# A decoder layer with eight experts: the gate threshold search with one clamping instruction a round, twenty held results, and the second half of the experts written out

## What is computed

```python
probs = jax.nn.softmax(xf @ Wr, axis=-1)              # 1792 tokens, 8 experts
topk_probs, topk_experts = jax.lax.top_k(probs, 2)
cap = 560                                             # max(ceil(1792*2*1.25/8), 1)
for e in range(8):
    mask = topk_experts == e
    gate = jnp.sum(jnp.where(mask, topk_probs, 0.0), axis=-1)
    g_masked = jnp.where(jnp.any(mask, axis=-1), gate, -jnp.inf)
    vals, idx = jax.lax.top_k(g_masked, cap)          # only the 560 largest gates stay
    g = jnp.where(jnp.isfinite(vals), vals, 0.0)
    h = jax.nn.relu(xf[idx] @ W1[e]) @ W2[e]          # 128 -> 512 -> 128
    y = y.at[idx].add(g[:, None] * h)
```

## Time and profile before

| | us |
|---|---|
| three runs | 1064.82, 1067.64, 1068.8 |
| median | 1067.64 |
| the profiled execution, its own time | 1067.1 |
| its span in the trace | 1065.4 |
| attention stages, up to the first product of part 0 | 865.6 |
| parts 0 to 63 | 101.2 |
| parts 64 to 127 | 77.7 |
| from the end of part 127 to the end of the span | 21.0 |

### The profile page before, as it was taken

How to read it: one execution, slowest core, us unless ns; L and a number is a source line. 1 busy time by engine, 2 the same in 40 slices (tenths; PEclk the granted TensorE clock), 3 DMA queues, 4 the chain that set the end, 5 groups by cost and what they waited for, 6 DMA issues and landing times.

```text
span 1065.4 us, 29427 instructions
## 1 busy us (share of the span) xinstructions
PE 991.5 (93%) x10672; PEld 801.4 (75%) x10672; DVE 726.2 (68%) x1428; ACT 633.0 (59%) x1026; POOL 354.7 (33%) x325
## 2 busy tenths in 40 slices
PE   6579999999999999999999999999977978999993
PEld 5345788877888778887788877888756767888993
DVE  3776777776777767777677777777721357767896
ACT  3214777777777777777777777777750033444551
POOL 7315333233332333323333233332200151117742
PEclk9757999999999999999999999999995568999997
DMA  4068556665566655666556665566401010004301
GB/s 95 0 129 176 126 111 139 150 142 111 108 143 145 142 112 108 143 145 143 111 108 144 144 143 109 108 148 143 103 2 42 1 40 20 21 1 158 126 34 35
DMA packets 41431, 109.57 MB, mean 103 GB/s; under 512 B 15075, under 2 KB 23590, under 8 KB 41382
## 3 DMA queue, kind: packets, MB, share of 16 engines
q1 hardware_dynamic: 41382, 108.93, 45.8%
HBM read 31.32 MB, written 0.97 MB: 30 GB/s over the span
## 4 chain that ended last, share of the span: by engine, by line
PE 79%; DVE 6%; POOL 5%; issue 5%; DMA 2%; SPq 1%; ACT 1%; POOLq 0%; DVEq 0%; ACTq 0%
PE psum L1050 16%; PE psum L1036 16%; PE psum L1100 12%; PE psum L1075 8%; PE psum L1084 8%; PE psum L1104 4%; PE psum L1167 3%; POOL OS_all L517 3%; PE psum L1195 2%; PE psum L1196 1%; PE psum L1197 1%; DMA arena<-gate_rows 1%; PE psum L1063 1%; PE psum L1168 1%; PE psum L1206 1%
## 5 line engine op out<-in xcount | busy, mean ns | idle before, releaser
L739 DVE TENSOR_REDUCE arena<-psum 128x1 f32<-128x500 f32 x672 | 445.4, 672 | 196.8 <-PE psum L1036 196.7
L562 ACT ACTIVATE arena<-psum 125x896 f32<-125x896 f32 x384 | 347.6, 915 | 98.4 <-PE psum L1050 90.3
L1036 PE MATMUL psum<-K_hi,Q_bd 128*128 128x500 f32 x672 | 321.9, 490 | 6.3 <-DVE arena L739 3.5
L461 POOL TENSOR_TENSOR arena<-arena,K_hi 128x500 fp32r<-128x500 f32 x96 | 123.9, 1292 | 395.8 <-ACT K_hi L577 394.8
L1050 PEld LDWEIGHTS psum<-Q_st,K_st 97*125 97x125 f32 x1536 | 220.7, 188 | 31.0 <-issue 11.2
L1050 PE MATMUL psum<-Q_st,K_st 97*125 97x224 f32 x1536 | 240.5, 279 | 3.1 <-issue 1.6
L1036 PEld LDWEIGHTS psum<-K_hi,Q_bd 128*128 128x128 f32 x672 | 130.4, 195 | 57.1 <-issue 28.3
L1100 PE MATMUL psum<-arena 125*25 125x168 f32 x3072 | 169.5, 310 | 0.2
L624 ACT ACTIVATE K_st<-psum 128x448 fp32r<-128x448 f32 x128 | 69.6, 544 | 89.8 <-PE psum L1197 89.4
L1104 PE MATMUL psum<-arena 125*9 125x56 f32 x3072 | 117.1, 213 | 0.0
L1104 PEld LDWEIGHTS psum<-arena 125*9 125x9 f32 x3072 | 94.4, 91 | 15.3
(11 more groups left out here) (245 smaller groups left out, 1104.1 us busy)
## 6 DMA issues: line engine op xcount, KB each, us to landing
K_st<-K_hi SPq DMA_DIRECT2D x256, 187.5 KB, 4.6
K_st<-arena SPq DMA_DIRECT2D x128, 187.5 KB, 3.4
arena<-in_ctx SPq DMA_DIRECT2D x32, 562.5 KB, 6.7
arena<-gate_rows SPq DMA_DIRECT2D x8, 896.0 KB, 4.5
arena<-in_L_ffn_W SPq DMA_DIRECT2D x16, 256.0 KB, 3.6
Q_st<-max_row SPq DMA_DIRECT2D x224, 0.5 KB, 1.7
arena<-K_st SPq DMA_DIRECT2D x12, 224.0 KB, 5.0
out<-x_all SPq DMA_DIRECT2D x4, 224.0 KB, 2.5
```

The costliest lines, as they stand in the source:

```text
L461: g.tensor_tensor(low.bitcast(F32R), low, K_hi[:, par, n * KB:n * KB + KB].bitcast(F32), ALU.subtract).then_inc(F["keys_low"], 1)
L562: a.activation(P2[c % NP].rearrange("p (n k) -> p n k", n=2), psum[0:CK, 2 + 2 * (c % 2):4 + 2 * (c % 2), 0:HQ // 2], ACT.Exp)\
L739: v.reduce_max(mx[:, n // NB, n % NB:n % NB + 1], bank_of(n)[:, 0:KB], AX.X).then_inc(F["piece_max_taken"], 1)
L1036: mm(bank_of(n)[:, 0:KB], Q_bd[:, p].rearrange("p h q -> p (h q)")[:, 128 * (n // NB):128 * (n // NB) + 128], K_hi[:, p, (n % NB) * KB:(n ...
```

## The change

**Constants.** `EARLY` is 13 and `BETWEEN` 49, so the gates are turned at part 13, and the rounds lie on parts 13 to 61: 17 rounds with two parts and 15 with one. There are `KEEP` = 20 places for results, four of them in a new array.

**Search.** `expert_rows` holds 4.0 instead of 1.0. A product of `ones` with the new array `level` fills 33 columns of bank 6 ahead of part 0 with minus four times 559.5; the product of round r is added to column r, so its sign says whether the count reaches the capacity. While the count is on its way, VectorE works out the two values that the candidate can take (`bounds`; two instructions in the first seven rounds, one in the next 23) into `low_high`, and when the sum is there, one instruction (max, then min with the two columns) gives the next candidate. The low parts of a round are moved one round later: behind the count of round r stand `low_parts(r - 1)`. The parts of the last round stand behind the count of equal gates, and the product for these (L1226, now L1273) stands behind part 63. Four small instructions that fill `signed` are new between the top two and the search.

**Experts.** All 32 units are written out on all engines. GpSimd splits the weights of experts 0 to 5 ahead of the first gating, those of expert 6 ahead of gating number 8 and of expert 7 ahead of number 18; SyncE loads the weights of experts 0 to 6 ahead of the gates. VectorE has no addition in units 16 to 18; the 30 additions of results 0 to 29 stand in units 19 to 31, two or three a unit, each behind one low part. The last two results are gated by VectorE itself, straight from PSUM, with no copy by ScalarE.

**End.** TensorE turns quad 0 ahead of the last `down` and quad 1 in the middle of it. VectorE's order is: statistics 0, gate and add result 30, scale 0, statistics 1, gate and add result 31, scale 1, statistics 2, scale 2, statistics 3, scale 3.

The core of the diff:

```diff
-EARLY, BETWEEN = 10, 46
+EARLY, BETWEEN = 13, 49
+KEEP = 20
+GATED = UNITS - 2
+WEIGHT = 4.0
+ADD_FROM = 19
...
+        more_results = at(128, KEEP - UNITS // 2, QC)
...
-            for e in range(NE - 2):
+            for e in range(NE - 1):
                 load_weights(e, e % 2)
...
-                if e in (1, 2):
-                    load_weights(NE - 3 + e, (NE - 3 + e) % 2)
+                if e == 1:
+                    load_weights(NE - 1, (NE - 1) % 2)
...
-            for e in range(NE // 2):
+            for e in range(NE - 2):
                 split_weights(e, e % 2, e // 2 + 1)
...
+            for n in range(GATED):
+                if n in (8, 18):
+                    e = NE - 2 if n == 8 else NE - 1
+                    split_weights(e, e % 2, e // 2 + 1)
+                e = n // NQ
+                pool.wait_ge(G_[e % 2], (e // 2 + 1) * 16)
+                pool.wait_ge(S4["result_copied"], n + 1 + PRIME)
+                g.tensor_tensor(held(n), held(n), gates[e % 2][:, n % NQ], ALU.mult).then_inc(S4["result_gated"], 1)
...
-                if not isinstance(u, int) or u >= UNITS // 2:
-                    act.wait_ge(S4["result_added"], u - (UNITS // 2 - 1) + PRIME)
-                a.activation(results[:, bass.ds(slot, 1)], bank[4 + p][:, 0:QC].unsqueeze(1), ACT.Copy).then_inc(S4["result_copied"], 1)
+                if u >= KEEP:
+                    act.wait_ge(S4["result_added"], u - KEEP + 1 + PRIME)
+                a.activation(held(u), bank[4 + u % 2][:, 0:QC], ACT.Copy).then_inc(S4["result_copied"], 1)
...
-            def count(op, where):
+            def count(op, where, bounds=None):
+                r = rounds[0]
                 v.tensor_scalar(gscr[:], G[:], where, 0.0, op, ALU.add, accum_out=cnt[:, 0:1]).then_inc(S4["counted"], 1)
-                for n in low_parts(rounds[0]):
+                if bounds:
+                    bounds()
+                for n in low_parts(r - 1) if r else ():
                     low_part(n // FC, n // FC, n % FC)
...
             for s in range(23):
-                bit, less = bits[:, s:s + 1], bits[:, min(s + 1, 22):min(s + 1, 22) + 1]
-                tot = count(ALU.is_ge, cand[:])
-                step(v.tensor_scalar(fac[:], tot, float(CAP), bit, ALU.is_ge, ALU.mult))
-                step(v.scalar_tensor_tensor((cand if s < 22 else thr)[:], fac[:], less, cand[:], ALU.subtract, ALU.add))
+                def bounds():
+                    last_of(v.tensor_scalar(low_high[:], offsets[:, s], cand[:], None, ALU.add))
+                tot = count(ALU.is_ge, cand[:], bounds)
+                step(v.tensor_scalar((cand if s < 22 else thr)[:], tot, low_high[:, 0:1], low_high[:, 1:2], ALU.max, ALU.min))
...
             v.tensor_copy(cnt[:, 1:2], pref[:, TT - 1:TT]).then_inc(S4["equal_counted"], 1)
+            for n in low_parts(ROUNDS - 1):
+                low_part(n // FC, n // FC, n % FC)
...
+            def gate(n):
+                dve.wait_ge(G_[1], 16 * (NE // 2))
+                dve.wait_ge(S4["result_made"], n + 1 + PRIME)
+                v.tensor_tensor(held(n), bank[4 + n % 2][:, 0:QC], gates[1][:, n % NQ], ALU.mult).then_inc(S4["result_gated"], 1)
+
+            def due(u):
+                return (u + 1 - ADD_FROM) * GATED // (UNITS - ADD_FROM) if u >= ADD_FROM - 1 else 0
+            for u in range(UNITS // 2, UNITS):
+                waiting = iter(range(due(u - 1), due(u)))
                 for f in range(FC):
-                    low_part(u, k, f)
...
+                    low_part(u, u, f)
+                    for n in islice(waiting, 1):
+                        add(n)
...
+            statistics(0)
+            gate(GATED)
+            add(GATED)
+            scale(0)
+            statistics(1)
+            gate(GATED + 1)
+            add(GATED + 1)
+            scale(1)
+            for n in range(2, NQ):
+                statistics(n)
+                scale(n)
...
-                        mm(bank[6][:, 0:1], expert_rows[:], cnt[:, 0:1], start=True, stop=True).then_inc(S4["total_made"], 1)
+                        mm(bank[6][:, rounds:rounds + 1], expert_rows[:], cnt[:, 0:1], start=False, stop=True, skip_group_check=True).then_inc(S4["total_made"], 1)
...
-                    if rounds == ROUNDS and u * FC + f == low_parts(ROUNDS - 1).stop + 3:
+                    if rounds == ROUNDS and u * FC + f == low_parts(ROUNDS - 1).stop + 1:
...
+            added(0)
             for f in range(FC):
                 down(UNITS - 1, UNITS - 1, f, 1)
...
+                if f == 1:
+                    added(1)
+            for n in range(2, NQ):
+                added(n)
```

More of the change, by code:

```diff
@@ L309, in bank_of @@
             return bank[0 if n == 0 else (n + 1) % 2]
-        def experts_after(eng, unit):
-            with eng.Fori(0, NE // 4) as i:
-                for k in range(2 * NQ):
-                    unit(i * (2 * NQ) + (UNITS // 2 + k), k)
         def has(b, ahead):
@@ L896, in count @@
                 rounds[0] += 1
[L897 to L906 removed]
+                dve.wait_ge(dve_step, done[0])
@@ L1210, in _, with added @@
             pe.wait_ge(S4["x_split"], NQ + PRIME)
+            mm(bank[6][:, 0:ROUNDS + 1], ones[:], level[:], start=True, stop=True).then_inc(S4["level_set"], 1)
             rounds = 0
-            for u in range(UNITS // 2):
+            def added(n):
+                pe.wait_ge(S4["result_added"], UNITS - NQ + n + 1 + PRIME)
+                for t in range(QT):
+                    last = t_.transpose(bank[(6, 7, 0, 1)[n]][0:TT, D * t:D * t + D], y_sum[:, n, TT * t:TT * t + TT], ident[:])
+                last.then_inc(S4["outputs_made"], 1)
+            for u in range(UNITS):
                 for f in range(FC):
```

109 lines of the change are left out of this document (50 added, 59 removed).

## The result

The changed kernel takes 1055.36 us (median of 4 runs, 1053.86 to 1056.22), against 1067.13 for the kernel before beside it: a ratio of 0.989, 95% interval 0.9867 to 0.9912. Timed once more with the last experiments it gave 1054.13 us and 0.990 (0.9868 to 0.9928). The forecast was 1056.5 in a range of 1053 to 1061.5.

What follows compares the result with a forecast made beforehand. TensorE alone was taken to bound parts 64 to 127, with the search costing it 26 us before; terms -1.0 -3.7 -3.6 +0.6 -3.5 +0 +0.5 +0.15 = -10.6 from 1067.1 gave 1056.5 us, range 1053 to 1061.5.

Steps and rivals of the forecast that it cites:

- stall ahead of turning: TensorE's wait before the gates are turned: three fewer steps behind the last low part, 2.49 to about 1.5 us, -1.0.
- clock behind it: Piece at 1.2 GHz behind the turning stall: taken to stay, 0; another -1.3 if the clock holds.
- rival 1: The early clock holds: no 1.2 GHz behind the 1.5 us stall, 1055.2 us; chance 0.14 with anything better.
- exponent to fraction: Search's change from exponent to fraction: stalls of 1.38 and 0.68 beside GpSimd's split and the slow-clock piece go, -3.7.
- steady rounds, with splits: Search rounds: 14 spared about 0.26 us each, -3.6; bounds held beside splits of experts 2, 3 and 4, +0.6.
- end of search: Stall of 2.02 us ahead of part 56 and its slow-clock piece go, 2.0 + 1.5 = -3.5.
- second half: Parts 64 to 127: TensorE's list has the same products, so nothing gained, 0; ends 0 and +4.
- tail: Behind part 127: early norms gain 4.3 us, added VectorE work and power waits give it back; +0.5.
- start of part 0: One new constant on GpSimd's opening list, which VectorE waits for: +0.15.
- Rivals 3 and 4: VectorE's additions beside GpSimd slow the second half: 1062.6 at worst (up to 1062: 0.09), or 1069.6 (0.04).
- rival 3: VectorE bounds units 21 to 29, paired additions 1.55 us each: +6, 1062.6 at worst; chance 0.09 up to 1062.
- the other 26 us of parts 0 to 63: The search's cost to TensorE beyond 75.2 us of products: stalls, 1.2 GHz pieces behind them, products of 32 counts.

Runs made afterwards that it cites:

- e5: Changed kernel with the product of the equal gates' sum two parts later, behind part 65 instead of 63: 1057.98 us (0.990).
- e2: Changed kernel with two more copies on VectorE between the top two's last step and the gathering of the gates, lengthening TensorE's stall: 1054.55 us (0.987).
- e8: Changed kernel with the tail of the kernel before (results 30 and 31 through ScalarE and GpSimd, added ahead of all norms): 1055.42 us (0.987).
- e3: Kernel before with one edit, GpSimd's split of expert 2's weights one unit later: 1062.38 us (0.995).
- e1: Changed kernel with VectorE's last steps reordered: statistics 2, scale 1, statistics 3, scale 2, scale 3: 1052.36 us (0.985).
- e4: Changed kernel with the low parts of a round computed in that same round again, clamp and bounds kept: 1055.53 us (0.987).
- e6: Changed kernel with a copy of the sum ahead of the clamp in each of the 30 rounds, low parts still one round later: 1054.17 us (0.987).
- e9: Changed kernel with a unit's additions all behind its four low parts instead of one behind each: 1059.15 us (0.993).
- e10: Changed kernel with e1's tail, gates turned at part 15 instead of 13, 47 parts instead of 49 for the rounds: 1052.48 us (0.9865).
- e7: Changed kernel with both the copy ahead of the clamp and the low parts in their own round: 1057.45 us (0.989).

## Why the prediction was right, step by step

| Step | Forecast | Measured, trace against trace |
|---|---|---|
| stall ahead of turning | -1.0 | -0.93 (10 parts in 15.16 and three more at 1.213, against 13 in 17.87) |
| clock behind it | 0 (rival 1: -1.3) | -1.32 |
| exponent to fraction | -3.7 | -3.71 |
| steady rounds, with splits | -3.6, +0.6 | -3.66 |
| end of search | -3.5 | -3.78 |
| second half | 0 | +0.09 |
| tail | +0.5 | +0.53 |
| start of part 0 | +0.15 | +1.88 |
| sum | -10.6 | -10.9 |

The steady rounds, worked out: before, turning to equal is 77.24 us, less 2.06 of stalls, 1.32 and 1.65 of slow pieces and 50 parts of 1.213, 11.56; now 69.76 less 51 parts, 7.90. The end: 8.77 us from the product of equal gates to part 64 before, 0.14 now, and four parts less, 4.85.

*The sum came out through errors that cancel, which is luck.* Parts 0 to 63 were to give 11.2 us and gave 13.4; the start of part 0 took most of the difference back. The clock held behind the stall left over, worth -1.3: rival 1, whose 1055.2 is nearer to the median of 1055.36 than the forecast is. The bounds beside splits cost nothing instead of 0.6: two of them were held, and had cover, as the timeline of DVE shows (0.43 and 0.42 instead of 0.22 to 0.23). And part 0 started 1.88 us later, not 0.15.

```profile
940.12 0.43 DVE L929 TENSOR_SCALAR low_high<-offsets,arena 128x2 f32<-128x2 f32 x1
942.48 0.42 DVE L929 TENSOR_SCALAR low_high<-offsets,arena 128x2 f32<-128x2 f32 x1
```

*The later start is no cost of the change.* TensorE's first product on x stood at 9.60 us in the first trace of before and at 10.75 in that of after:

```profile
9.60 0.98 PE L964 MATMUL psum<-ident,arena 112*128 112x112 f32 x4 [2.78 <-SPq L342]
```
```profile
10.75 0.98 PE L1004 MATMUL psum<-ident,arena 112*128 112x112 f32 x4 [3.74 <-SPq L348]
```

In the other traces it lies anywhere between (9.94 and 10.40 in the two others with the code of before, 9.87 in the second of after, 9.69 in e5), so it isn't the new constant. But the arrival of x explains 1.15 of the 1.88 us at most, and part 0 doesn't follow it: e2 has x at 10.41 and part 0 at 865.18, e8 has 9.87 and 869.32. The rest is the attention, which no kernel here touches: from x to part 0 it took 855.99 and 856.72 us in the two first traces, and 854.77 to 859.45 over all fourteen. The prediction's "nothing ahead of part 0 but one small constant" also leaves out the product of `level` (L1251, 0.61 us). It costs nothing, since it falls into the wait for GpSimd's first split: from the end of the products with `Wr_sb` to part 0 it is 1.28 us before and 1.22 after. The rows of part 0, before and after:

```profile
865.59 0.71 PE L1195 MATMUL psum<-K_hi,K_st 128*128 128x448 f32 x1 [1.27 <-issue]
```
```profile
867.47 0.74 PE L1235 MATMUL psum<-K_hi,K_st 128*128 128x448 f32 x1 [0.75 <-POOL K_st L512]
```

So no cost of the change shows here, not even the 0.15. What was missing is that the start of part 0 moves by up to 4 us between executions (865.18 to 869.32), and the first 13 parts by 1.4 more with the clock.

*Where the steps were right for the stated reason*: GpSimd's split held VectorE at the change from exponent to fraction (e3, for 1.7 of the stalls' 2.06 us; the 1.65 of the slow piece is not shown to be theirs); the low part queued behind the wait made the stall at the end (e5); the tail's two waits, to 0.1 us (e1, e8).

*Where the reason was too narrow*: the steady rounds. The prediction wanted low parts one round later and a single clamp together for its -3.6; e4 and e6 show that either alone gives most of it (of 3.5 us, the clamp alone 2.7 and the delay alone all).

*Where a term was right and its ground thin*: the second half. Rivals 3 and 4 had 0.13 together. Their mechanism is real (e9: up to 1.53 us an addition in a row, and +1.8 us in the second half against rival 3's worst of +6), and what keeps it away is the placing one by one, which the prediction priced no better than pairs (1.7 us for a slot with an addition, against 1.55 each in a pair). It took TensorE's 2.85 us of room as enough; in e9 the additions used it up and made a low part 0.88 us late.

*The clock*: the prediction booked 1.3, 1.65 and 1.5 us of slow pieces as parts of its terms, as if the stalls owned them. The two traces of the unchanged kernel agree with that; e3 has none behind 2.49 and 2.02 us, e5 none behind 2.03, e2 none behind 2.04. So a removed stall gives its own length, and a slow piece only in some executions. The prediction's list of what makes up the other 26 us of parts 0 to 63 also leaves out a slow piece: the one at part 0 itself, 6.0 us long in the first trace of either kernel, which the change doesn't touch.

## What to carry to other kernels

Look for what is queued behind a wait before asking how long the wait is: twice here a single instruction in the wrong place (low part 62, a scale behind its own statistics) cost 2 us. Where two edits open the same short interval, undo them one at a time and together; each may be enough alone, and then neither's share can be read from one undo. Spread instructions that another engine can hold between others that it doesn't: the same additions were about a quarter dearer in a row.

## What the runs showed of the hardware that was not expected

- The slow pieces of TensorE's clock come and go between executions behind the same stall (2.48 or 2.49 us: two of three; 2.02 to 2.04: two of five; 1.38 with 0.68: two of two; 1.51 or 1.52: one of nine), and the first rise after the stretch of small work ahead of part 0 came 3.0 to 6.4 us into it. Each piece behind a stall costs 1.3 to 1.7 us, more than several edits of this change. The stretch from 781 to 791 us ran at 1.2 GHz in e10 and at 2.4 in e1.
- One DMA issue on SyncE in the opening (weights WkA) took 0.51 us in one execution and 1.68 in another with the same work around it. The length of this issue and the arrival of x go together over all fourteen traces: where the issue took 0.46 to 0.84 us, TensorE's first product on x stood at 9.60 to 9.94 us, and where it took 1.07 to 1.68, at 10.20 to 10.75. x is issued ahead of it; which of the two follows from the other, or both from a third thing, was not tried.
- VectorE stood 0.28 us ahead of the first gating of the tail in the changed kernel, for no reason that the profile shows ("issue"). The pause is gone in the runs with two or thirty instructions more on its list (e2, e6, e7) and in e10, which only moves some; the tail of e2 is 0.37 us shorter, that of e10 0.37 us shorter than e1's. Why was not tried.

```profile
1036.18 0.62 DVE L963 TENSOR_TENSOR OS_all<-psum,arena 128x448 f32<-128x448 f32 x1 [0.28 <-issue]
```
